# Cross attentions of a two-layer decoder: the value product in fp32 instead of three fp16 products of halves

## The reference

```python
def xattn(q, ctx, mask):                     # q (8,256,256), ctx (8,77,256)
    qh = split(q @ w_q.T + b_q)              # (8,16,256,16)
    kh = split(ctx @ w_k.T + b_k)            # (8,16,77,16)
    vh = split(ctx @ w_v.T + b_v)
    scores = einsum('bhtd,bhsd->bhts', qh, kh) / sqrt(16)
    attn = softmax(masked(scores), -1)       # (8,16,256,77)
    out = einsum('bhts,bhsd->bhtd', attn, vh)
    return merge(out) @ w_o.T + b_o
x = layernorm(x + xattn(x, ctx, mask))
```

## Time and profile before

| | us |
|---|---|
| median of 3 runs | 1293.64 |
| lowest and highest | 1292.46, 1300.71 |
| the profiled execution | 1291.09 |
| its span in the trace | 1289.3 |
| TensorE, VectorE, ScalarE, GpSimd busy in the span | 1087.8, 961.6, 704.9, 388.9 |

### The profile page before, as it was taken

How to read it: one execution, slowest core, us unless ns; L and a number is a source line. 1 busy time by engine, 2 the same in 40 slices (tenths; PEclk the granted TensorE clock), 3 DMA queues, 4 the chain that set the end, 5 groups by cost and what they waited for, 6 DMA issues and landing times. The chain is left out here.

```text
span 1289.3 us, 30260 instructions
## 1 busy us (share of the span) xinstructions
PE 1087.8 (84%) x10763; PEld 881.4 (68%) x10763; DVE 961.6 (75%) x2254; ACT 704.9 (55%) x1459; POOL 388.9 (30%) x538
## 2 busy tenths in 40 slices
PE   4899989999987699986269999389999569999696
PEld 3578878778776577774257777378787447777485
DVE  7587877878875488884938883569998538888497
ACT  2454444444443355552637775368788525655484
POOL 5122222222220355551130000423331225555232
PEclk9899999999999799995559999699999879999799
DMA  6000000100000500005245431300000000000011
GB/s 257 5 10 2 10 12 2 71 3 2 2 2 2 187 23 22 11 9 227 107 135 172 171 108 49 120 17 26 24 9 9 0 24 23 11 21 9 34 50 50
DMA packets 34072, 65.35 MB, mean 51 GB/s; under 512 B 7590, under 2 KB 23334, under 8 KB 30886
## 3 DMA queue, kind: packets, MB, share of 16 engines
q1 hardware_dynamic: 32422, 59.62, 13.2%
q0 software_dynamic: 1536, 4.20, 1.0%
HBM read 43.03 MB, written 12.39 MB: 43 GB/s over the span
## 5 line engine op out<-in xcount | busy, mean ns | idle before, releaser
L953 POOL TENSOR_TENSOR ca_z<-ca_z,ca_top 128x308 f32<-128x308 f32 x128 | 92.7, 724 | 129.8 <-DVE ca_top L1082 129.5
L389 ACT ACTIVATE wa_probs<-wa_scores,wa_minus_top 128x192 f32<-128x192 f32 x256 | 83.3, 437 | 80.6 <-DVE wa_minus_top L477 80.6
L1025 ACT ACTIVATE ca_pth<-ca_turned 77x512 f16<-77x512 f32 x128 | 75.9, 593 | 59.0 <-PE ca_turned L1209 58.4
L348 POOL TENSOR_TENSOR wa_q<-wa_by_cos,wa_by_sin 128x256 f32<-128x256 f32 x32 | 23.4, 732 | 266.3 <-DVE wa_by_sin L472 266.3
L1209 PE MATMUL ca_turned<-ident,ca_probs 128*77 128x128 f32 x512 | 84.1, 287 | 20.6 <-ACT ca_probs L1017 19.5
L400 ACT ACTIVATE wa_pth<-wa_turned 128x384 f16<-128x384 f32 x128 | 58.4, 506 | 73.5 <-PE wa_turned L696 73.5
L1200 PE MATMUL ca_scores<-ca_km,ca_q 128*128 128x308 f32 x256 | 89.6, 433 | 6.0 <-ACT ca_q L998 5.7
L1087 DVE SCALAR_TENSOR_TENSOR ca_ptl<-ca_turned,ca_pth 77x512 f16<-77x512 f32 x128 | 86.7, 677 | 2.6 <-ACT ca_pth L1025 2.6
L1017 ACT ACTIVATE ca_probs<-ca_z 128x308 f32<-128x308 f32 x128 | 58.2, 455 | 44.8 <-POOL ca_z L953 43.8
L621 PE MATMUL wa_scores<-wa_xh,wa_wh 128*128 128x256 f16 x256 | 70.5, 275 | 11.7 <-DVE wa_wl L456 9.7
L477 DVE TENSOR_REDUCE wa_minus_top<-wa_scores 128x2 f32<-128x384 f32 x128 | 62.3, 549 | 21.1 <-PE wa_scores L684 18.9
(11 more groups left out here) (332 smaller groups left out, 3677.0 us busy)
## 6 DMA issues: line engine op xcount, KB each, us to landing
ex_stage<-in_ew SPq DMA_DIRECT2D x16, 1024.0 KB, 7.0
slots<-slots_zeros SPq DMA_DIRECT2D x10, 512.0 KB, 5.3
ca_xs<-tokens SPq DMA_DIRECT2D x16, 256.0 KB, 2.3
ex_xe<-slots SPq DMA_DIRECT2D x11, 320.0 KB, 3.3
slots<-ex_y SPq DMA_DIRECT2D x9, 320.0 KB
wa_x_stage<-in_xt SPq DMA_DIRECT2D x8, 256.0 KB, 3.0
tokens<-in_x SPq DMA_DIRECT2D x1, 2048.0 KB, 14.8
ca_w<-in_xw SPq DMA_DIRECT2D x2, 1024.0 KB, 5.6
```

The source lines that it names most:

```text
L389: ins = act.activation(probs[2 * (u % 2) + t][:, h, t * WINDOW:t * WINDOW + SPAN], s_bank[i][:, t * SPAN:(t + 1) * SPAN], ACT.Exp, bias=mi ...
L953: pool.tensor_tensor(z[k][:], z[k][:], top[:, k].unsqueeze(2).broadcast_to((P, UH, CTX)), ALU.subtract).then_inc(shift, 1)
L1025: act.activation(pth[k][0:CTX], t_bank[k][0:CTX], ACT.Copy, scale=PSCALE).then_inc(probs_high, 1)
```

## The change

The turned probabilities are kept once, in fp32 (`pt`), by the same ScalarE copy. The values stay in fp32 (`v`, now with two buffers, the column of ones in it). `weigh` makes one fp32 product for each head. The halves and what makes them go: `value_high` on ScalarE, `value_low` and `probs_rest` on VectorE. What waited for the low half now waits for the ScalarE copy.

```diff
-        v = sb("v", [P, CH, CD])
-        vh = [sb(f"vh{k}", [P, CH, CD + 1], F16) for k in range(2)]
-        vl = [sb(f"vl{k}", [P, CH, CD + 1], F16) for k in range(2)]
+        v = [sb(f"v{k}", [P, CH, CD + 1]) for k in range(2)]
...
-        pth = [sb(f"pth{k}", [P, UH * P], F16) for k in range(2)]
-        ptl = [sb(f"ptl{k}", [P, UH * P], F16) for k in range(2)]
+        pt = [sb(f"pt{k}", [P, UH * P]) for k in range(2)]
...
-            def value_high(b, par):
-                wait_read(act, [("value", 0)], b)
-                act.activation(vh[par][0:CTX, :, 0:CD], v[0:CTX], ACT.Copy, scale=SCALE).then_inc(v_high, 1)
-
...
-                    act.activation(pth[k][0:CTX], t_bank[k][0:CTX], ACT.Copy, scale=PSCALE).then_inc(probs_high, 1)
+                    act.activation(pt[k][0:CTX], t_bank[k][0:CTX], ACT.Copy).then_inc(probs_kept, 1)
...
-                if not first(b):
-                    dve.wait_ge(v_low, b)
-                dve.tensor_tensor(v[0:CTX], shared[bank][0:CTX, 0:DIM].rearrange("p (h d) -> p h d", h=CH),
+                dve.tensor_tensor(v[par][0:CTX, :, 0:CD], shared[bank][0:CTX, 0:DIM].rearrange("p (h d) -> p h d", h=CH),
                                   rows[0:CTX, 0].rearrange("p (h d) -> p h d", h=CH), ALU.add).then_inc(free[bank], 1)
-
-            def value_low(b, par):
-                dve.wait_ge(v_high, b + 1)
-                dve.scalar_tensor_tensor(out=vl[par][0:CTX, :, 0:CD], in0=v[0:CTX], scalar=SCALE,
-                                         in1=vh[par][0:CTX, :, 0:CD], op0=ALU.mult, op1=ALU.subtract).then_inc(v_low, 1)
...
-            def probs_rest(b, c):
-                k = c % 2
-                dve.wait_ge(probs_high, b * UNITS + c + 1)
-                dve.scalar_tensor_tensor(out=ptl[k][0:CTX], in0=t_bank[k][0:CTX], scalar=PSCALE, in1=pth[k][0:CTX],
-                                         op0=ALU.mult, op1=ALU.subtract).then_inc(probs_low, 1)
-
...
                         mask_scores(*two_on)
-                    probs_rest(b, c)
-                    if two_on:
                         take_maximum(*two_on)
...
                 k, t = c % 2, c // (UNITS // TPB)
-                pe.wait_ge(probs_low, b * UNITS + c + 1)
+                pe.wait_ge(probs_kept, b * UNITS + c + 1)
...
                 for h in range(UH):
                     head = UH * (c % (UNITS // TPB)) + h
-                    cols = slice(h * P, (h + 1) * P)
-                    for n, (a, x) in enumerate(((pth[k], vh[par]), (pth[k], vl[par]), (ptl[k], vh[par]))):
-                        ins = pe.matmul(o_bank[t][:, head, 0:CD + 1], a[0:CTX, cols], x[0:CTX, head],
-                                        start=(n == 0), stop=(n == 2))
+                    ins = pe.matmul(o_bank[t][:, head, 0:CD + 1], pt[k][0:CTX, h * P:(h + 1) * P], v[par][0:CTX, head],
+                                    start=True, stop=True)
```

More of the change, by code:

```diff
@@ L862, in cross_attention @@
         key_masked = sem("key_masked")
-        v_high = sem("v_high")
-        v_low = sem("v_low")
         token_sum = sem("token_sum")
@@ L871, in cross_attention @@
         probs_t = sem("probs_t")
-        probs_high = sem("probs_high")
-        probs_low = sem("probs_low")
+        probs_kept = sem("probs_kept")
         weighted = sem("weighted")
@@ L1032, in batch @@
                         step(b + d, (par + d) % 2, kind, i, bank, uses)
-                    if c == 2 and after:
-                        value_high(b + 1, 1 - par)
-            act.wait_ge(ones, 1)
             for kind, i, bank, uses in CA.prologue():
                 step(0, 0, kind, i, bank, uses)
-            value_high(0, 0)
             power(0, 0)
@@ L1047, in _ @@
             for k in range(2):
-                dve.memset(vh[k][:, :, CD:CD + 1], SCALE)
-                ins = dve.memset(vl[k][:, :, CD:CD + 1], 0.0)
+                ins = dve.memset(v[k][:, :, CD:CD + 1], 1.0)
             ins.then_inc(ones, 1)
@@ L1128, in batch @@
                         norm.apply(dve, b - 1, 1, at(X, (b - 1) * TPB + 1))
-                    if c == 2 and after:
-                        value_low(b + 1, 1 - par)
             for kind, i, bank, uses in CA.prologue():
@@ L1134, in _ @@
                     value(0, 0, bank, uses)
-            value_low(0, 0)
             if not additive:
@@ L1206, in turn_probs @@
                 if not (first(b) and c < 2):
-                    pe.wait_ge(probs_low, b * UNITS + c - 1)
+                    pe.wait_ge(probs_kept, b * UNITS + c - 1)
                 for h in range(UH):
@@ L1213, in weigh @@
                 k, t = c % 2, c // (UNITS // TPB)
-                pe.wait_ge(probs_low, b * UNITS + c + 1)
+                pe.wait_ge(probs_kept, b * UNITS + c + 1)
                 if c == 0:
-                    pe.wait_ge(v_low, b + 1)
+                    wait_read(pe, [("value", 0)], b)
+                    if first(b):
+                        pe.wait_ge(ones, 1)
                 if c % (UNITS // TPB) == 0 and not first(b):
```

## The result

The change makes the kernel slower. Its median is 1328.43 us in 4 runs (1319.22 to 1333.67), beside 1293.24 of the kernel before in 4 runs (1292.46 to 1300.71): a ratio of 1.0244, with a 95% interval of 1.0203 to 1.0285. The forecast was 1329. The profiled execution took 1328.09 us and its span is 1326.4, 37.1 us over that of before.

What follows compares the result with a forecast made beforehand. TensorE, nearly full, was taken as the bound, going from 18.35 to 21.2 us a batch. Twelve periods +34.2, first batches +3.8, last +1.0, start -0.9, end -0.6 made +37.5: 1329 us, range 1316 to 1348.

Steps and rivals of the forecast that it cites:

- What bounds: Attention periods: TensorE has 16.5 us of work in 18.35, rising to 21.2; VectorE's busy time falls to about 10.9.
- Eight rows: `weigh`, per unit: four fp32 products, each a weight load and a stream, replace twelve fp16 products.
- the rival of four loads: `weigh`: each fp32 product needs four loads, 16 rows a unit, giving 1440 us; chance 0.02.
- 0.112 a row: `weigh` on TensorE: the load of 128 fp32 columns decides, 0.112 us a row, bounded by neighbours at 0.108 to 0.112.
- The block of 0.90: `weigh` on TensorE: eight rows of 0.112 make 0.90 us against 0.31, +0.59 a unit and +4.7 a batch.
- The waits go: Attention periods: TensorE's standing 1.85 us a batch is filled, including waits for query copy (0.51) and exponential (0.57).
- The ends: Outside the periods: first batches +3.8, last batches +1.0, start -0.9, end -0.6 us.
- The first batch: First batch of each attention: TensorE's work goes from 15.1 to 19.2 us, +1.9 each, twice +3.8.
- The last batch of the second attention: Last batch: +0.5 us for each attention; at its end `probs_rest` no longer precedes residual and norm, -0.3 each.
- The start: Start of first attention: without `value_low` ahead, the mask's limits can run before the scores come, -0.9 us.
- The rival of a falling clock: Attentions: TensorE's clock falls; one tenth of some 330 us at half clock adds about 30, 1360 us; chance 0.04.
- The sum: Whole kernel: periods +34.2 and the ends' terms make +37.5 us, giving 1329 us.

Runs made afterwards that it cites:

- the rests kept: Changed kernel with `probs_rest` put back on VectorE, written to a tile nothing reads, `weigh` and transposes waiting for it: 1326.28 us, ratio 1.0227.
- the wide stream: Changed kernel with each fp32 product of `weigh` streaming 32 columns instead of 17: 1324.0 us, ratio 1.0226.
- 32 fp16 rows: Changed kernel with probabilities and values kept once in fp16, each head's product done eight times into the same sum: 1322.5 us, ratio 1.0202.

## Why the prediction was right

**What bounds.** It said that TensorE works 16.5 us of a period of 18.35 and becomes the bound. After, TensorE is busy for 123.80 of 123.80 us, and putting VectorE's 24 us back changes nothing. Held. VectorE's own figure was off: 10.9 us of a period were forecast and 71.64 / 6 = 11.9 measured, since the time that a rest held the engine (0.60) was taken off a busy sum in which operations overlap. Nothing hung on it.

**Eight rows.** x8 in the trace, 1024 in the kernel. Held, and with it the rival of four loads falls. In this trace one fp32 product is two rows and 0.224 us where an fp16 one is 0.0255, 8.8 times. The page of the Trainium skill cited there (FP8 and Floating Point Precision, TensorE Precision Notes) has fp32 as four passes. Four passes at the measured price of an fp16 product would be 0.10, by estimate. With loads of 128 columns and 17 streamed the measured row decides, not the count of passes.

**0.112 a row.** The spacing is 0.112, with 17 columns as with 32. Held.

**The block of 0.90.** This term was mis-sized. It is 0.81: the first load is covered by the stream before it, so the block pays seven spacings and 0.03. The growth is 0.50 a unit, not 0.59, and 4.0 a batch, not 4.7. TensorE's work is then 16.5 + 4.0 = 20.5 where 21.2 was forecast, and the period came out at 20.64. For the twelve periods that is 27.5 us, not 34.2.

**The waits go.** Both are gone, though what grew beside them was 0.50 each instead of 0.59, against 0.51 and 0.57; the exponential's chain also lost its 0.60 of `probs_rest`. That loss wasn't needed: with the rests kept the period is 20.64 as well. Only 20.64 - 20.5, about 0.1, is left over TensorE's sum. Held.

**The ends.** Forecast was 3.8 + 1.0 - 0.9 - 0.6 = 3.3 for all that isn't a period; measured is 36.7 - 27.5 = 9.2. Most of it goes with the clock. From the clocks of whole attentions, the kernel before stood at half clock for about 34 us in the two, the kernel after for 52 and the wide stream for 29 (an estimate: length x (1 - clock) x 2); in all three the periods hold 1.00, so this time lies at the ends. The wide stream's attentions are 28.2 us longer than those of before, so with 27.5 in the periods the ends cost 0.7 at nearly the same clock, less than the 3.3.

The first batch shows the same. It grew by 2.0 in the first attention (19.77 to 21.74) and by 4.3 in the second (17.3 to 21.6, at a clock of 0.86 where before it was 1.00). In the wide stream's execution it takes 20.26 at 0.92. So some 2.8 us more at half clock cost 1.35, and at full clock the batch would take about 18.6 (an estimate): +1.3, which is the 15.1 of TensorE's work and seven times the true 0.50. The +1.9 was too high by the mis-sized block, and that the first attention's 2.0 matches it is luck. The last batch of the second attention, from its first transposes to the end of the norm, grew by 1.1 (24.58 to 25.71); 0.2 was forecast, and the wide stream has 24.40. The start went the forecast way: in the first attention the first masking now comes 0.90 us after the first score (429.82 to 430.72) and not 2.28 (432.23 to 434.51), 1.4 less where 0.9 was forecast.

The rival of a falling clock thus showed in small, at the ends of the attentions and not in the periods. No run tells why the clock fell there in one execution and not in the other.

**The sum.** 37.5 was forecast, 37.1 measured in the profiled executions, and 35 between the medians. That it fits this well is luck: the periods were taken 6.7 us too high, the ends at equal clock 2.6 too high, and the longer time at half clock gave 8.6 back, with 0.4 from the stages outside. The experiments whose period is 20.64 or 20.68 at both attentions (the rest kept, the wider stream, 32 fp16 rows) lie 27 to 29 us over the medians of before beside them. The chosen range (1316 to 1348) held both; its lower part was added up a little too wide, since 1329 - 4 - 5 is 1320 and not 1318.

**What ScalarE pays for fp32.** Costed at nothing: the copy takes 592 ns, 593 before. Held.

## What to carry to other kernels

Count a product with a small moving side by its weight loads: here an fp32 one is two loads of 0.112 us, 8.8 fp16 products, so one in the place of three adds to TensorE's time, and where TensorE is nearly full, as here, that outweighs the relief elsewhere. Work taken from the second-busiest engine counts only as long as the first doesn't grow: try the two halves of such a trade apart, since here one was worth -21 us (1297.09 to 1276.35) and the other +48 (1276.35 to 1324.0, with the wide stream as the kernel after that was run in the same series). For a block of n short rows take n - 1 spacings and a covered first one, not n. And before a forecast is called good by its total, compare the time at half clock of the two executions: here it was worth 8.6 of 37.1 us.

## What the runs showed of the hardware

- The time of an fp32 load goes with its columns: 0.112 us for 128 and 0.056 to 0.060 for 64. The stream beside it is free at 17 and at 32 columns.
- Going between products on 128 and on 64 columns costs about 0.09 us on the way in and 0.15 on the way out. It was seen in one experiment alone; what makes it isn't known.
- GpSimd's subtraction of 128x308 fp32 values goes from 0.70 to 1.21 or 1.39 us when VectorE's 128x256 fp32 scaling of SBUF to SBUF begins in its middle, and to 0.80 when the scaling had begun 0.16 us ahead of it. Beside VectorE's rest, which reads the turned bank (L1087), it keeps its 0.70. Moving the scaling ahead of it takes the long ones away.
- The stretches at half clock lie in other places from one execution to the next, also where the order of TensorE's work is the same: the first batch of the second attention is at 0.86 in the kernel after and at 0.92 with the wide stream. The four executions after have mean clocks of 0.920, 0.919, 0.932 and 0.913 and spans of 1326.4, 1327.1, 1317.5 and 1331.9 us: the lower the clock, the longer the span. What makes the clock fall at the ends of an attention wasn't tried and stays open.
